# Clipped cross attention with keys on the partitions, and new slot tables around it

## The reference

```
def _L2_xattn_ref(x, context, mask, Wq, Wkv, Wo, bo):
    H, DH = (16, 64); SCALE = DH ** (-0.5)
    q = x @ Wq                              # (b, 128, 1024)
    k, v = split(context @ Wkv, 2)          # (b, 128, 1024) each
    sim = einsum('bhid,bhjd->bhij', q, k) * SCALE
    sim = where(mask[:, None, None, :], sim, -max)
    sim = clip(sim, -5.0, 5.0)
    attn = softmax(sim, axis=-1)
    out = einsum('bhij,bhjd->bhid', attn, v)
    return out(b, i, 1024) @ Wo + bo
```

## Time and profile before

| | us |
|---|---|
| median of 3 runs | 2006.95 |
| lowest and highest | 2003.97, 2009.08 |
| the profiled execution | 2010.01 |
| its span | 2008.3 |
| TensorE busy in the span | 1766.3 |
| DVE busy | 1399.8 |
| ACT busy | 1329.1 |
| POOL busy | 826.4 |

### The profile page before, as it was taken

The page is one execution under the profiler, slowest core; times in us unless marked ns, Lnnn a source line. Parts: engine busy times, 40 slices in busy tenths (PEclk is TensorE's granted clock), DMA queues, the critical chain, the costliest instruction groups (busy, mean ns, idle before and its releaser), DMA issues. The chain is left out here.

```text
span 2008.3 us, 40721 instructions
## 1 busy us (share of the span) xinstructions
PE 1766.3 (88%) x13945; PEld 1312.3 (65%) x13945; DVE 1399.8 (70%) x3927; ACT 1329.1 (66%) x5380; POOL 826.4 (41%) x951
## 2 busy tenths in 40 slices
PE   6998988889998998998979999517899996899998
PEld 5757955536886866875645787214577775467776
DVE  4686788998433677789899543875976664885665
ACT  2596589828774587569937876434766664776666
POOL 2471047717332363026826433012643343653335
PEclk9999999989999999989989999756999998899999
DMA  6000000000001000000000000200000000000000
GB/s 242 1 1 2 1 1 2 2 1 2 1 2 37 1 2 2 1 1 1 2 1 1 1 2 33 86 0 14 1 2 1 1 1 25 1 2 1 1 1 11
DMA packets 6984, 24.81 MB, mean 12 GB/s; under 512 B 752, under 2 KB 3440, under 8 KB 6128
## 3 DMA queue, kind: packets, MB, share of 16 engines
q1 hardware_dynamic: 6768, 22.09, 2.9%
HBM read 21.04 MB, written 1.05 MB: 11 GB/s over the span
## 5 line engine op out<-in xcount | busy, mean ns | idle before, releaser
L1414 POOL TENSOR_TENSOR a_probs<-a_probs,a_rinv 128x512 f32<-128x512 f32 x352 | 365.8, 1041 | 324.5 <-DVE a_rinv L1251 321.4
L1057 ACT ACTIVATE a_probs<-bank,a_negmax 128x128 f32<-128x128 f32 x896 | 327.2, 453 | 26.2 <-DVE a_negmax L1230 26.0
L1414 POOL TENSOR_TENSOR c_probs<-c_probs,c_rinv 128x512 f32<-128x512 f32 x192 | 199.9, 1041 | 195.2 <-DVE c_rinv L1251 193.0
L899 PEld LDWEIGHTS bank<-const,a_probs 128*128 128x128 f32 x1408 | 161.8, 147 | 131.3 <-issue 112.6
L1057 ACT ACTIVATION_READ_ACCUMULATOR a_probs<-bank,a_negmax 128x1 f32 x896 | 239.2, 294 | 0.0
L899 PE MATMUL bank<-const,a_probs 128*128 128x128 f32 x1408 | 231.7, 292 | 3.7 <-DVE a_probs_t L1258 1.8
L1424 POOL TENSOR_TENSOR a_rstd<-a_ve,neg_half 128x1 f32<-128x1 f32 x128 | 70.2, 549 | 349.6 <-DVE a_ve L1309 349.6
L1230 DVE TENSOR_REDUCE a_negmax<-bank 128x4 f32<-128x512 f32 x224 | 151.8, 680 | 19.3 <-PE bank L867 13.3
L867 PE MATMUL bank<-a_kz,a_qk 32*128 32x512 f32 x512 | 149.9, 662 | 4.6 <-POOL a_kz L1392 2.6
L1258 DVE COPY a_probs_t<-bank 128x512 f32<-128x512 f32 x192 | 131.4, 685 | 29.3 <-PE bank L899 29.3
L885 PE MATMUL bank<-a_xt,w_L_ffn 128*128 128x128 f32 x1024 | 136.9, 277 | 0.0
(11 more groups left out here) (268 smaller groups left out, 4451.6 us busy)
## 6 DMA issues: line engine op xcount, KB each, us to landing
w_L_ffn<-in_L_ffn SPq DMA_DIRECT2D x1, 3184.0 KB, 15.2
w_L_xattn<-in_L_xattn SPq DMA_DIRECT2D x1, 2112.0 KB, 22.7
w_L_xattn<-in_L_xattn SPq DMA_DIRECT2D x1, 2050.0 KB, 9.5
a_xt<-in_xT SPq DMA_DIRECT2D x3, 512.0 KB, 3.6
a_x<-in_x SPq DMA_DIRECT2D x3, 512.0 KB, 5.1
a_ct<-in_ctxT SPq DMA_DIRECT2D x3, 512.0 KB, 4.5
w_L_attn<-in_L_attn SPq DMA_DIRECT2D x1, 1345.5 KB, 17.9
w_L_attn<-in_L_attn SPq DMA_DIRECT2D x1, 1157.0 KB, 6.1
```

Source lines behind the costliest of these rows:

```text
L899: mm = pe.transpose(bank[:, j * S:(j + 1) * S], Pb[:, n % PB, j * S:(j + 1) * S], ident)
L1057: op = act.activation(p, bank_of("scores", n)[:, j * width:(j + 1) * width], ACT.Exp, bias=negmax[:, n % PB, j:j + 1], accum_out=rsum[:, n ...
L1414: pool.tensor_tensor(p, p, along(rinv[:, n % PB, 0:heads], 512 // heads), ALU.mult).then_inc(sems["norm_done"], 1)
```

## The change

In L2_xattn the scores are computed with K as the stationary operand, so keys lie on the partitions and queries in the columns. Q64 has the layout of K64 and no zeros; each matmul uses 64 rows, even heads the upper half and odd heads the lower. Two units are computed together, one with the four even and one with the four odd heads, into two banks. The clip is one tensor_scalar whose upper bound is a value per partition; the mask is loaded with keys on the partitions. One exponential covers the four heads of a unit, without a sum. V65 holds V with a 65th column of ones per head, and the product of the exponentials (stationary) with it gives, queries on the partitions, the unnormalised output and in the last column the sum. DVE inverts the sums out of PSUM and multiplies into U, and TensorE transposes U, two heads at a time, into the layout of a_ot. The stage "norm" is empty for this layer.

The tables change as well: EARLY, LEAD, REST, BANKS and PT_ACT for most kinds.

```diff
 EARLY = {
-    "mqa": [("q0", 6, "dve"), ("q1", 6, "dve"), ("kv", 5, "dve")],
+    "mqa": [("q0", 6, "dve"), ("q1", 4, "dve"), ("kv", 5, "dve")],
-    "h8p": [("qk", 9, "act"), ("v", 1, "dve")],
-    "h8r": [("qk", 9, "dve"), ("v", 5, "dve")],
-    "moe": [("router", 26, "dve"), ("gateT", 6, "act"), ("biases", 3, "dve")],
+    "h8p": [("qk", 10, "act"), ("v", 1, "dve")],
+    "h8r": [("qk", 9, "dve"), ("v", 6, "dve")],
+    "moe": [("router", 26, "dve"), ("gateT", 6, "act"), ("biases", 2, "dve")],
-    "h64c": [("q0", 9, "act"), ("q1", 7, "act"), ...
+    "h64c": [("q0", 11, "act"), ("q1", 7, "act"), ...
 LEAD = {
-    "scores": {... "h64m": 5, "ffn": 4},
-    "max": {... "h8p": 6, "h8r": 6, "h64m": 4, "ffn": 4},
-    "front": {"all": 3, "h8": 5, "h8p": 4, "h8r": 5, "lin": 2},
-    "norm": {"all": 2, "h8": 4, "h8p": 3, "moe": 1, "ffn": 3},
+    "scores": {... "h64m": 6, "ffn": 4},
+    "max": {... "h8p": 5, "h8r": 6, "h64m": 5, "ffn": 4},
+    "front": {"all": 3, "h8": 5, "h8p": 4, "h8r": 5, "lin": 2, "h64c": 2, "h64m": 4},
+    "norm": {"all": 2, "h8": 3, "h8p": 3, "moe": 1, "ffn": 3},
 REST = {
-    "turn": {"all": 6, "mqa": 5, "h8p": 7, "moe": 7, "h64c": 5, "h64m": 7},
-    "take": {"all": 6, "mqa": 5, "h8p": 7, "moe": 7, "h64c": 5, "h64m": 7},
+    "turn": {"all": 6, "mqa": 5, "h8": 7, "h8p": 7, "moe": 7, "h64c": 5, "h64m": 7},
+    "take": {"all": 6, "mqa": 5, "h8": 7, "h8p": 7, "moe": 7, "h64c": 5, "h64m": 7, "ffn": 8},
 BANKS = {
-    "h64c": {"scores": (0, 1, 2, 3), "second": (4,), "use": (6, 7), "values": (5,)},
+    "h64c": {"scores": (0, 1, 2, 3), "second": (4, 5), "use": (6, 7), "values": (6, 7)},
-    "ffn": {"scores": (0, 1, 2), "second": (4, 5), "use": (6, 7)},
+    "ffn": {"scores": (0, 1, 2), "second": (3, 4), "use": (5, 6, 7)},
-PT_ACT = {"h8": (3,), "h8p": (0, 1, 3), "h8r": (1, 3), "h64c": (1, 2, 3)}
+PT_ACT = {"h8": (3,), "h8p": (0, 1, 3), "h8r": (1, 2, 3), "h64c": (1, 2, 3)}
...
@@ load of the mask
-                    of = of.rearrange("a n -> (a n)").partition_broadcast(P) if name == "mask_bk1" else of.rearrange("a p n -> p (a n)")
+                    if name == "mask_bk1":
+                        return nc.sync.dma_start(mask_u8[:, :], of.rearrange("a (g p) -> p (a g)", p=P), allow_slow_non_contiguous=True)
+                    of = of.rearrange("a p n -> p (a n)")
@@ TensorE, scores
                         elif kind == "h64c":
+                            bank_free("scores", n + 1)
                             for j in range(4):
-                                mm = pe.matmul(bank[:, j * S:(j + 1) * S], Qz[:, plan.ring(s, 2), 2 * i + j // 2, j % 2, :], K64[:, plan.ring(s, 2), 2 * i + j // 2, :], start=True, stop=True)
+                                for odd in range(2):
+                                    half = slice(64 * odd, 64 * odd + 64)
+                                    mm = pe.matmul(bank_of("scores", n + odd)[:, j * S:(j + 1) * S], K64[half, plan.ring(s, 2), 2 * i + j, :],
+                                                   Q64[half, plan.ring(s, 2), 2 * i + j, :], start=True, stop=True)
+                                    if j == 3 and odd == 0:
+                                        mm.then_inc(sems["scores_ready"], 1)
@@ TensorE, second
-                        if kind in SOFTMAX:
+                        if kind == "h64c":
...
+                            pe.wait_ge(sems["exp_done"], plan.count("exp", n))
+                            for j in range(4):
+                                h = 8 * (i // 2) + 2 * j + i % 2
+                                mm = pe.matmul(bank[:, j * 65:(j + 1) * 65], Pb[:, n % PB, j * S:(j + 1) * S], V65[:, plan.ring(s, 2), h, :], start=True, stop=True)
+                        elif kind in SOFTMAX:
@@ TensorE, values (odd units alone)
                             for j in range(4):
-                                h = 4 * i + j
-                                mm = pe.matmul(value_bank[64 * (j % 2):64 * (j % 2) + 64, (j // 2) * S:(j // 2 + 1) * S],
-                                               V64[:, plan.ring(s, 2), 0, h * 64:(h + 1) * 64], pt[:, j * S:(j + 1) * S], start=True, stop=True)
+                                mm = pe.transpose(value_bank[:, j * S:(j + 1) * S], U[:, plan.ring(s, 2), 4 * (i // 2) + j, :, :].rearrange("p o d -> p (o d)"), ident)
@@ ACT: Q out of PSUM, exponentials, output
-                            for j in range(2):
-                                op = act.activation(Qz[64 * j:64 * j + 64, plan.ring(s, 2), 4 * half:4 * half + 4, j, :],
-                                                    heads_view(bank[64 * j:64 * j + 64, :], 4), ACT.Copy, scale=0.125)
+                            op = act.activation(Q64[:, plan.ring(s, 2), 4 * half:4 * half + 4, :], heads_view(bank[:, :], 4), ACT.Copy, scale=0.125)
+                                act.activation(Pb[:, n % PB, :], Pb[:, n % PB, :], ACT.Exp).then_inc(sems["exp_done"], 1)
-                                    op = act.activation(p, p, ACT.Exp, accum_out=rsum[:, n % PB, j:j + 1])
-                            op = act.activation(OT[:, plan.ring(s, 2), 2 * i:2 * i + 2, :], heads_view(value_bank[:, 0:2 * S], 2), ACT.Copy)
+                            op = act.activation(OT[:, plan.ring(s, 2), 4 * (i // 2):4 * (i // 2) + 4, :], heads_view(value_bank[:, :], 4), ACT.Copy)
@@ DVE: clip, reciprocal and multiply
-                            dve.scalar_tensor_tensor(heads_view(Pb[:, n % PB, :], 4), heads_view(bank[:, :], 4), -5.0, over(clip_hi[:, b, :], 4),
-                                                     ALU.max, ALU.min).then_inc(sems["moved"], 1)
+                            dve.tensor_scalar(Pb[:, n % PB, :], bank[:, :], -5.0, clip_hi[:, b:b + 1], ALU.max, ALU.min).then_inc(sems["moved"], 1)
+                            if kind == "h64c":
+                                sums = heads_view(bank_of("second", n)[:, 0:260], 4)
+                                heads = U[:, plan.ring(s, 2), 4 * (i // 2):4 * (i // 2) + 4, i % 2, :]
+                                link(dve.reciprocal(rinv[:, n % PB, 0:4], sums[:, :, 64]))
+                                dve.tensor_tensor(heads, sums[:, :, 0:64], along(rinv[:, n % PB, 0:4], 64), ALU.mult).then_inc(sems["pt_dve"], 1)
+                                return
```

More of the change, by code:

```diff
@@ L50 @@
     "exp": SOFTMAX,
[L51 removed]
+    "norm": ("mqa", "h64m") + H8,
     "silu": ("moe", "ffn"),
@@ L158, in __init__ @@
             claims += [("scores", m) for m in self.due["scores"].get(n, [])]
-            claims += [("values", m) for m in self.due["values"].get(n, []) if self.kind(self.units[m][0]) not in H8 or self.units[m][1] == 3]
+            claims += [("values", m) for m in self.due["values"].get(n, []) if self.gathers(m)]
             claims += [("second", m) for m in self.due["second"].get(n, [])]
@@ L192, in placed @@
             now = max(m - LEAD[stage].get(kind, LEAD[stage]["all"]), at, before + 1)
-            if stage == "scores" and kind in H8:
+            if stage == "scores" and kind in H8 + ("h64c",):
                 now = at if i % 2 else max(now, at + 1)
@@ L244, in count, with gathers @@
         if stage == "values":
-            return sum(self.kind(s) in SOFTMAX and (self.kind(s) not in H8 or i == 3) for s, i in self.units[:n + 1])
+            return sum(self.gathers(m) for m in range(n + 1))
         return sum(self.kind(s) in STAGES[stage] for s, _ in self.units[:n + 1])
+    def gathers(self, n):
+        s, i = self.units[n]
+        kind = self.kind(s)
+        return kind in SOFTMAX and (i == 3 if kind in H8 else i % 2 == 1 if kind == "h64c" else True)
     def copier(self, n):
```

47 lines of the change are left out of this document (30 added, 17 removed), and 4 rows, old and new, of the table LEAD.

## The result

The changed kernel takes 1985.12 us (median of 4 runs, 1980.86 to 1988.28) against 2008.01 us (4 runs, 2003.97 to 2010.83): the ratio is 0.9886, 95% interval 0.9860 to 0.9912, a gain of 22.9 us. The forecast was 1978 us and its range 1960 to 1997.

What follows compares the result with a forecast made beforehand. The prediction took TensorE's passes to bound L2_xattn and DVE to bound L3_attn. -23 - 7 - 1 + 2 = -29 took the profiled 2010.0 us to 1981; with the median 3 us lower, 1978 us, range 1960 to 1997.

Steps and rivals of the forecast that it cites:

- Products at the pace of their loads: L2_xattn products with V: 8 passes take 0.89 us, as in a projection, 3.56 us per batch.
- rivals A: L2_xattn products: narrow passes are free of the load's pace, 27 us more gained, 1951 us; chance 5%.
- B: L2_xattn products: narrow passes cost 0.17 us each, load and product in turn, +29 us, 2007 us; chance 4%.
- Scores in pairs: L2_xattn scores: 64-row matmuls run two at a time; a pair of units costs 1.12 us, 2.24 per batch.
- E: L2_xattn scores: the pairs of 64-row matmuls don't form, +1.8 us per batch, 2007 us; chance 2%.
- L2_xattn -23: TensorE in L2_xattn: 1.56 us less per batch, 25 us over 16 batches, less 2 us for waits at turn ends.
- DVE in the middle of the chain, and the banks, at nothing: L2_xattn: DVE's reciprocal and multiply before the transposes, and ten bank claims per batch, cost nothing; at worst 29 and 32 us.
- rival D: L2_xattn: DVE's 0.9 us trip between two TensorE groups is bare for each unit, +58 us, 2036 us; chance 6%.
- L3_attn -7: L3_attn: a copy moves from DVE to ACT, batch 8.8 to 8.3 us, 7 steady batches in two turns.
- The tables elsewhere -1: Table edits in the other stages move waits about where TensorE is about 91% busy: -1 us, bounds -10 and +10.
- rival C: Tables: no gain in L3_attn, L2_attn pays 5 us for ACT, later turns cost 6; 1997 us, chance 10%.
- The start +2: Before the loop: the mask's first load, 1024 one-byte pieces instead of 128 of 1024 bytes, costs 2 us more.

Runs made afterwards that it cites:

- Experiment 4: Changed kernel with V65 padded to 128 columns per head, so products move 128 columns instead of 65: 1987.56 us, ratio 0.9895 to the kernel before.
- experiment 3: Changed kernel with L2_xattn scores issued as four even heads, then four odd, instead of alternating: 2001.30 us, ratio 0.9973 to the kernel before.
- Experiment 8: Changed kernel with all four units' scores of an L2_xattn batch in one group of 32 matmuls, not two of 16: 1987.29 us, ratio 0.9892.
- 10: Experiment 8's kernel with the transposes of U and their copy one slot later: 1977.60 us, ratio 0.9867 to the kernel before.
- Experiments 5: Changed kernel with one of two copies per batch of L2_attn and L3_attn back from ACT to DVE: L3_attn batch 9.2 to 9.3 us.
- 6: Changed kernel with the second normalisation of L3_attn (the write of c_lh) one slot later: L3_attn batch 8.9 us.
- 7: Changed kernel with the V projection of L2_attn and L3_attn five slots ahead instead of six: L3_attn batch 8.4 us.
- 9: Changed kernel with V of L2_attn and L3_attn five slots ahead and c_lh written by POOL instead of DVE: 1988.79 us, ratio 0.9922.
- experiment 12: Changed kernel with the mask loaded three more times before the loop, in one-byte pieces: the loop begins 6.8 us later.
- experiments 1 to 4: Ratios to the kernel before: it with the new tables alone 0.9993; changed kernel with old tables 0.9901, scores not alternating 0.9973, products 128 wide 0.9895.
- 11: Changed kernel with the edits of 9 and 10 together: 1977.30 us, ratio 0.9865 to the kernel before.

## Why the prediction was right, and what in it was not

The mechanism on TensorE and the direction were right; most terms of the sum were too large. Point by point:

- **Products at the pace of their loads: right.** 8 passes fill 0.84 us and pass 0.05 on to the next group, 0.89 together. Experiment 4 excludes rivals A and B. (The prediction took its lower bound of 0.06 us per pass for what the 60 cycles of the Trainium skill's page "TensorE: Matmul & The Clock Gate", section "Back-to-back issue gap", would give; 60 cycles are 0.025 us at the 2.4 GHz level, by this estimate from the page's figure well under that bound. The products came by the load's pace, so nothing hung on it.)
- **Scores in pairs: right,** E is excluded by experiment 3.
- **L2_xattn -23: too large, by the switches of TensorE.** The step that failed is the sum per batch, 1.56 us, of which 1.17 came. It gave a pair of units 1.12 us and the products behind them 0.89. Measured are 1.09 and 0.09 for the way in, which is 0.06 more, and 0.99 for the products (0.94 and 0.05 on the next group), which is 0.10 more. Twice per batch that is 0.33 of the missing 0.39 us; the other 0.06 are in the output projection, 550.52 to 552.37 = 1.85 us where before it took 1.79. The trace of before had the way in and the way out; what I did not look for is that the first pass behind a switch also has its load exposed (first to second pass 0.21 us in the changed kernel's scores). Experiments 8 and 10 price a full round trip: 14.17 - 13.80 = 0.37 us. Only three of the seven steps between output projections are at 14.17 us; with the edges of the stage, 8 x 1.17 = 9.4 us per turn become 8.1 to 9.6.
- **DVE in the middle of the chain, and the banks, at nothing: right** for the steady batches of the changed kernel, where TensorE waits for neither. The margin is small: the multiply ends at 558.42 us, and the transposes that need it begin at 558.53. In the last batches of the first turn TensorE does wait, 1.5 us for that multiply and 0.8 for ACT's copy to a_ot; the prediction took off 2 us for both turns. Experiment 8 shows how near rival D was: with less on TensorE between product and transposes, 0.36 us per batch are bare.
- **L3_attn -7: the wrong step.** I took 0.5 us for 7 steady batches in each turn. Only three of the seven intervals are steady (8.8 us; the others 10.3 to 15.4 before), which makes 3 us of it; and the interval fell by 0.14 us to 8.66, not by 0.5. DVE did lose a copy, 0.60 us of its interval from start to next start. But it got back 0.24 us of work with the add of c_qk, which now runs beside a POOL multiply (0.65 us for 0.42), 0.17 in short waits behind the reciprocals and 0.05 in smaller ones. And c_lh took 1.18 us for 0.34 in both kernels. Experiments 5, 6, 7 and 9 put the batch at 9.2, 8.9, 8.4 and 8.1 us by moving these two instructions and the copy (in 6 a transpose's wait comes in as well). The stage is 2.1 us shorter in each turn; the steady intervals give 0.4 of it, the one behind them 0.2, and the rest lies ahead of the second output, where kernels with the same tables differ by up to 2 us. The rest of the loss, from 8.66 down to TensorE's 7.8, is what I had called "some loss in the handing over" without looking who takes it.
- **The tables elsewhere -1: right as a sum** (-1.4 us for all tables, with -4 to +1), by parts that cancel: rival C, in a small form. Its 5 us in L2_attn for ACT's copy did not come; that layer's batch is shorter, 7.77 us for 7.92.
- **The start +2: wrong.** The price of the pieces was right, 2.3 us per load, though by luck: it came from a guessed quarter of a mean packet's busy time, while in experiment 12 the engines are busy for only 0.20 of the time that the pieces take. But I had taken the load that they replace to be short. It took as long, and its wait of 1.8 us was in the earlier trace rows. Why 128 pieces of 1024 bytes took 3.4 us was not looked into.

So the sum by medians was -23 + 2 for the rewrite, measured -20, and -8 for the tables, measured -1. The first agreement is partly luck, since in the profiles L2_xattn gives only 16.2 to 17.8 us of it and the start nothing. That the profiled spans differ by just the 29 us of the forecast is chance too: the four executions of the changed kernel alone lie 7.4 us apart.

Much of that scatter goes with the granted clock. Of the 11 executions of the kernel before beside experiments 9 to 12, the fastest, 1997.31 us, has a mean of 0.954 and the slowest, 2009.74, of 0.944 (the correlation over the 11 is -0.96; over the 23 beside experiments 1 to 4 it is -0.83). One place in the traces: the same step of L0_xattn's last batches, first in the changed kernel, then in experiment 4 and before the change:

```profile
151.40:159.40 8.00, 5.83 (x69) 4.87 (x69) 6.48 (x20) 4.07 (x21) 5.32 (x7) 1.00 0.00 0
280.00:345.00 65.00, 56.84 (x466) 37.69 (x467) 55.42 (x138) 63.51 (x297) 43.77 (x52) 0.87 0.01 1
```

```profile
151.40:161.80 10.40, 8.33 (x68) 7.33 (x68) 6.68 (x20) 4.17 (x21) 5.74 (x7) 0.67 0.00 0
```

```profile
151.58:161.53 9.95, 7.78 (x71) 6.26 (x71) 6.17 (x19) 4.48 (x21) 4.41 (x6) 0.83 0.00 0
```

At 1.00, the 2.4 GHz level, the step takes 8.0 us, at 0.67 (part of it at 0.5, the 1.2 GHz level) 10.4, and before, at 0.83, 9.95: this one step is 1.95 of the 2.3 us by which L0_xattn is shorter in the first turn. The second row of the first kernel lies in its L1_attn, at 0.87; the same stretch before the change:

```profile
280.00:345.00 65.00, 53.44 (x473) 35.23 (x471) 57.27 (x137) 63.53 (x293) 46.38 (x53) 0.93 0.01 2
```

In this stretch TensorE is at the lower level more often with the new tables (0.82 to 0.89 in all kernels that have them, 0.93 and 0.95 in the two that have not), and busy for 56.8 us instead of 53.4, while the stage itself hardly moves, since ACT has 63.5 of its 65 us in both. In the second turn (910 to 970 us) the two sets overlap, 0.82 to 0.94 against 0.94 twice. Over the whole span the 12 executions with the tables alone have 0.936 to 0.944, the 23 of the kernel before 0.943 to 0.951. What puts the engine there, and how much of the tables' missing 7 us it costs, was not settled.

The Trainium skill's page "SBUF — State Buffer", section "Who interferes with whom", says that a DVE instruction with two SBUF inputs contends with a GpSimd instruction that reads SBUF, that one in a two-port mode contends with GpSimd too, and that whichever issues first holds the shared ports for its whole length while the other is blocked. The runs agree in kind: the add of two SBUF tiles takes 0.65 us beside a multiply and 0.43 alone, and c_lh, started 0.17 us ahead, takes 0.32. That c_lh, with one tensor in SBUF, runs in a two-port mode no run shows but by its being held up. They differ in detail: with a lead of 0.06 us c_lh still lost, and it then ended only 0.08 us behind the multiply's record, less than its own 0.34. By this rule I could have asked of the moved V take where the add behind it would land; I weighed none of it.

## What to carry to other kernels

When every pass brings a new stationary operand of 128 columns, count loads, not moving columns: passes of 65 and of 128 cost the same here, to 0.05 us per batch. Count each change of TensorE between full and half arrays at both ends and add the exposed load of the first pass behind it; putting two such groups into one (11.5 us between experiments 9 and 11) was worth more here than all the tables. Before calling a layer's interval steady, print the intervals; and when work leaves a full engine, look at what its neighbours on that engine will now run beside.
